# Score matmuls issued in front of the maxima matmuls within each attention step

## The chip, the cores and the metric

The kernel runs on one core of one Trainium2 chip. The metric is the time of one execution on the device in microseconds (us); the number given for a kernel is the median of several runs. TensorE is written PE below (its weight loads PEld), VectorE DVE, ScalarE ACT, GpSimd POOL, SyncE SP.

## What is computed

The reference is one layer of 16 sequences of 256 tokens, width 128, in float32: half a feed-forward block, attention, half a feed-forward block, each behind a layer norm and added to its input.

```python
x = x + 0.5 * ffn(layernorm(x))
x = x + attention(layernorm(x))        # 16 heads of 8 channels
x = x + 0.5 * ffn(layernorm(x))

# attention, for a batch of 256 tokens
scores = einsum('bhqd,bhkd->bhqk', q, k) * 8 ** -0.5
attn = softmax(scores, axis=-1)
o = einsum('bhqk,bhkd->bhqd', attn, v)
return einsum('bse,fe->bsf', o, Wo) + bo

# ffn, weights ternary with a scale per output
h = silu(lin(x, w1)) * lin(x, w2)
h = gelu(lin(h, h1)); h = gelu(lin(h, h2))
return lin(h, w3)
```

## The kernel before

All tokens stay in the tile `X`. The program has three stages: feed-forward over four blocks of 1024 tokens, attention over 16 batches of 256 tokens (one sequence each), feed-forward again. Each engine has its own instruction list, written out by hand, and they meet at semaphores only. Engines take their instructions in the order in which they are written.

**The softmax in two passes.** To subtract a row's maximum, the kernel computes the scores twice. The maxima matmuls (`max_scores`, line 1098) give scores with queries on the partitions; DVE reduces them to maxima (`max_unit`, line 828, the reduction at line 832). The negated maxima of a batch are turned by two PE transposes (`max_rows`, line 1136), and split into a high and a low part by ACT (line 657) and DVE (`split_max`, line 836, semaphore `m_lo`). The score matmuls (`scores`, line 1109) compute the scores a second time with keys on the partitions, and add the maxima through a selector matmul into the same bank; ACT takes the exponential (line 647). `weigh` (line 1121) multiplies the probabilities with the values.

**Units and steps.** A batch has 16 maxima units and 16 score units, each one PSUM bank of 128 x 512: two heads. A maxima unit is 2 matmuls (line 1104), a score unit 4 (lines 1116, 1118, twice). They contract over 32 rows only, one of four row groups ("lanes") of the array. `attend` for batch b has 16 steps u. Step u holds maxima unit u of the next batch, b + 1, and score unit u - 4 of batch b, or for u below 4 unit u + 12 of batch b - 1 (`in_step`, line 278). The lane of both is worked out from the unit's number, so that an even step and the odd step behind it use four different lanes: two for maxima, two for scores.

**Other work of a step.** At u = 3, 7, 11 and 15 stand two `weigh`s, 16 matmul records over all 128 rows. At u = 1 stands `max_rows`, at 3 `transpose_o`, at 5 `project_out`, at 13 `tokens_of_o`. An even batch up to 12 also has `project_v` at u = 9; an odd batch up to 11 has `transpose_att` at 7, `project_q` at 9 and `project_k` at 11, for the batches to come. All of this stands behind the matmuls of the step. All other steps, the even ones, hold nothing else.

**Banks and waits.** The maxima share three banks (`A_BANKS`), the scores three others (`B_BANKS`), so a maxima unit waits for DVE's reduction three units before (`max_done`, line 1102), a score unit for ACT's exponential three units before (`exp_done`, line 1113). At u = 4 score unit 0 also waits for `m_lo`. `transpose_att` waits for `att_added` (line 1330), which DVE's `add_att` (line 865) gives at its step 6. `max_rows` waits for `o_norm` of DVE's `scale_o` and for `max_twice` of POOL's `max_again` (line 444), which follows the last maxima of the batch.

DVE's order in a step is maxima unit, then the rest (`attend`, line 957): `split_max` at 2, layer norm's `normalise` at 3 in odd batches (line 770), `add_att` at 6, the norm statistics at 7 to 11 in even batches, `norm_o` at 14, `scale_o` at 15. ACT's order is in `attend`, line 663.

Of the kernel before, what the change touches and what calls it, by code (L numbers as in the profile page):

```python
# [53 lines left out]
A_BANKS = ((0, 1, 5) * 5 + (0,), (5, 1, 0) * 5 + (5,))  # L54
B_BANKS = ((2, 3, 7) * 5 + (2,), (7, 3, 2) * 5 + (7,))
ENTRY_BANKS = (0, 3, 1, 2) * 4
# [9 lines left out]
def macaron_kernel(nc, x, w_ffn, w_att, s12, sg, s3, bqk, bv, bo, eye, sel, low_rows, out):  # L66
# [11 lines left out]
    with ctx:  # L78
# [176 lines left out]
        def wait(eng, s, v):  # L255

            if not isinstance(v, int) or v > 0:
                eng.wait_ge(s, v)
# [10 lines left out]
        def a_unit(u):  # L269

            jj, lane = u // 2 % 2, 2 * (u // 4 % 2) + u % 2
            return u // 8, jj, lane

        def b_unit(v):

            return v // 8, v // 2 % 2, 2 * (v // 4 % 2) + v % 2

        def in_step(u, prev, own=True):


            at = [(0, u - SKEW)] if own else []
            if prev:
                at.append((1, u - SKEW + UNITS))
            return [(d, v) for d, v in at if 0 <= v < UNITS + 4]

        def used_last(banks, prev, u):


            before = prev + banks[:u]
            return next((d for d in range(1, len(before) + 1) if before[-d] == banks[u]), u + 1)  # L290

        def q_of(ring):

            return QK[:, RING - 1 - ring, 0, :, :]

        def k_of(ring):

            return QK[:, RING - 1 - ring, 1, :, :]
# [710 lines left out]
        def _(pe):  # L1009
# [88 lines left out]
            def max_scores(b, par, bb, u, banks, prev):  # L1098

                qt, jj, lane = a_unit(u)  # L1100
                rows = slice(32 * lane, 32 * lane + 32)
                wait(pe, max_done, UNITS * b + u - used_last(banks, prev, u) + 1)
                for i in range(2):
                    ins = MM(bank[banks[u]][:, SEQ * i:SEQ * i + SEQ],  # L1104
                             q_of(2 * par + bb)[rows, 2 * jj + i, P * qt:P * qt + P],
                             k_of(2 * par + bb)[rows, 2 * jj + i, :], start=True, stop=True)
                ins.then_inc(a_mm, 1)

            def scores(b, par, bb, v):

                jj, kt, lane = b_unit(v)
                rows = slice(32 * lane, 32 * lane + 32)
                wait(pe, exp_done, UNITS * b + v - used_last(B_BANKS[bb], B_BANKS[1 - bb], v) + 1 + CREDIT)
                for i in range(2):
                    dst = bank[B_BANKS[bb][v]][:, SEQ * i:SEQ * i + SEQ]
                    MM(dst, k_of(2 * par + bb)[rows, 2 * jj + i, P * kt:P * kt + P],  # L1116
                       q_of(2 * par + bb)[rows, 2 * jj + i, :], start=True, stop=False)
                    ins = MM(dst, SEL[rows, 2 * jj + i, :], m_parts[rows, bb, :], start=False, stop=True)  # L1118
                ins.then_inc(b_mm, 1)

            def weigh(b, par, bb, g, kt):


                pe.wait_ge(exp_done, UNITS * b + 4 * g + 2 * kt + 2 + CREDIT)
                if kt == 0 and g == 0:
                    wait(pe, o_out, b)
                for h in range(4):
                    col = BLOCK * (4 * g + h) + V_AT - VW * (g % 3)
                    ins = MM(bank[4][32 * h:32 * h + 32, SEQ * (g // 3):SEQ * (g // 3) + SEQ],  # L1129
                             V[par][:, VROW * (2 * bb + kt) + col:VROW * (2 * bb + kt) + col + BLOCK],  # L1130
                             probs[:, (4 * g + 2 * kt + h % 2) % 8, SEQ * (h // 2):SEQ * (h // 2) + SEQ],
                             start=kt == 0 and g in (0, 3), stop=kt == 1 and g >= 2, tile_position=(0, 32 * h))
                if kt == 1:
                    ins.then_inc(pv_mm, 1)

            def max_rows(b, bb):
                pe.wait_ge(max_twice, 2 * b + 2)
                for qt in range(2):
                    ins = T.transpose(bank[6][:, P * qt:P * qt + P],  # L1139
                                      neg_max[:, bb, qt, :], EYE[:, :])  # L1140
                ins.then_inc(m_T, 1)
# [9 lines left out]
            def transpose_o(b):  # L1151
                pe.wait_ge(o_norm, b + 1)
                for qt in range(2):
                    ins = T.transpose(bank[6][:, P * qt:P * qt + P], o_nat[:, qt, :], EYE[:, :])
                ins.then_inc(on_T, 1)
# [116 lines left out]
            def attend(b, pair, par, bb, prev=True, prev2=True, own=True, more=True, steps=UNITS,  # L1272
                       ahead=None, v_pair=None):

                npar, nbb = (par, 1) if bb == 0 else (1 - par, 0)
                ppar, pbb = (par, 0) if bb == 1 else (1 - par, 1)
                if more:  # L1280

                    of = pair + 1 - nbb
                    pe.wait_ge(qk_loaded[2 * npar + nbb], LOADS // 2 * (of - npar) + LOADS)
                def rows_of_max():
                    if prev2:
                        pe.wait_ge(o_norm, b - 1)
                    elif prev:
                        pe.wait_ge(v_set, pair + 2)
                    max_rows(b, bb)

                for u in range(steps):
                    if u == 0 and own and not prev:
                        pe.wait_ge(q_full, 1)
                        pe.wait_ge(k_full, 1)
                    if more:
                        max_scores(b + 1, npar, nbb, u, A_BANKS[nbb], A_BANKS[bb] if prev else ENTRY_BANKS)
                    for d, v in in_step(u, prev, own):
                        at = (b - d, par, bb) if d == 0 else (b - d, ppar, pbb)
                        if d == 0 and v == 0:
                            pe.wait_ge(m_lo, b + 1)  # L1300
                        if v < UNITS:
                            scores(*at, v)
                        if d == in_step(u, prev, own)[-1][0] and u == 1 and own:
                            rows_of_max()
                        if v >= 7 and v % 4 == 3:
                            weigh(*at, v // 4 - 1, 0)
                            weigh(*at, v // 4 - 1, 1)
                    if u == 1 and own and not prev:
                        pe.wait_ge(x_added, NB + CREDIT)
                        rows_of_max()  # L1310
                    if u == 3 and prev2:
                        if own:
                            pe.wait_ge(m_lo, b + 1)
                        else:
                            pe.wait_ge(o_norm, b - 1)
                        transpose_o(b - 2)
                    if u == 5 and prev2:
                        project_out(b - 2)
                    if u == UNITS - 1 and not more and own:
                        transpose_x(XN1, 0, 1)  # L1320
                        transpose_x(XN1 + 1, 1, 5)
                    if u == 9 and v_pair is not None:

                        if prev2:
                            pe.wait_ge(att_added, b - 1)
                        pe.wait_ge(m_lo, b + 1)
                        project_v(v_pair, 6)
                    if u == 7 and ahead is not None:
                        if prev2:
                            pe.wait_ge(att_added, b - 1)  # L1330
                        pe.wait_ge(m_lo, b + 1)
                        pe.wait_ge(v_set, pair + 2)
                        transpose_att(ahead, 0, 6)
                    if u == 9 and ahead is not None:
                        project_q(ahead, 6)
                    if u == 11 and ahead is not None:
                        pe.wait_ge(q_full, ahead)
                        project_k(ahead, 6)
                    if u == TOKENS and own and prev:

                        if ahead is not None:
                            pe.wait_ge(k_full, ahead)
                        elif v_pair is not None:
                            pe.wait_ge(v_set, v_pair + 1)
                        elif prev2:
                            pe.wait_ge(att_added, b - 1)
                        tokens_of_o(b - 1)
# [68 lines left out]
```

## Time and profile before

| | |
|---|---|
| median of 3 runs | 638.17 us (636.6 to 639.28) |
| the profiled execution's own time | 636.52 us |
| its span, first to last instruction | 634.7 us |
| granted TensorE clock, mean over the span | 0.986 |
| PE busy, of the span | 94% |
| ACT busy | 74% |
| DVE busy | 69% |
| POOL busy | 15% |

The profile is of one execution. The span is 1.8 us shorter than that execution's time, and that execution is 1.65 us below the median. Attention lies between about 219 and 445 us of the span. A timeline row gives a group of instructions: start in us from the span's start, length in us, engine, source line, operation, what it writes and reads, partitions x elements, the count, and in brackets the idle time of the engine before it with what ended it. Rows of PE overlap, as matmuls of different lanes run at the same time.

### The profile page before, as it was taken

The numbers are of one execution on the slowest core, as the hardware profiler recorded it, in microseconds if no ns is written. First come the engines' busy times: TensorE is split into PE (matmuls) and PEld (weight loads), VectorE is DVE, ScalarE is ACT, GpSimd is POOL, SyncE is SP. The second block draws the span as 40 slices with busy tenths as digits, with TensorE's granted clock in tenths as the row PEclk, the third lists the DMA queues.
The fourth block names the chain that finished last, engine by engine and source line by source line (L and its number), as shares of the span: only waits on it lengthen the run. The fifth ranks groups of instructions, "written<-read, shape, count | busy, mean of one in ns | idle before, by whom it ended". The sixth has DMA issues, their size and how long they took to land.

```text
span 634.7 us, 12980 instructions
## 1 busy us (share of the span) xinstructions
PE 597.0 (94%) x4452; PEld 437.7 (69%) x4452; DVE 436.8 (69%) x1034; ACT 466.7 (74%) x793; POOL 94.7 (15%) x258
## 2 busy tenths in 40 slices
PE   1959999999999999999999999999899999999996
PEld 0738878878776675656656565666578878788785
DVE  4845485667835687979889898896385666855742
ACT  2746796787875568787878878787587877977964
POOL 2702001021010311222222222012001020020000
PEclk9979999999999979999999999999899999999999
DMA  8200000000034073434437062400000001000011
GB/s 287 69 2 2 0 1 1 2 0 0 1 133 133 24 242 124 144 136 133 165 104 263 36 229 106 162 2 2 3 2 0 1 1 35 0 6 27 1 33 35
DMA packets 36674, 41.97 MB, mean 66 GB/s; under 512 B 2448, under 2 KB 27280, under 8 KB 36624
## 3 DMA queue, kind: packets, MB, share of 16 engines
q1 hardware_dynamic: 36624, 41.31, 19.3%
q8 instruction: 31, 0.51, 0.3%
q14 instruction: 19, 0.16, 0.1%
HBM read 22.42 MB, written 18.87 MB: 65 GB/s over the span
## 4 chain that ended last, share of the span: by engine, by line
PE 76%; DVE 8%; issue 7%; POOL 3%; ACT 3%; DMA 2%; POOLq 0%; SPq 0%; DVEq 0%; ACTq 0%
PE bank L1021 48%; PE bank L1129 7%; PE bank L1104 6%; PE bank L1116 3%; PE bank L1118 2%; DVE neg_max L832 2%; PE bank L1161 2%; PE bank L1086 1%; PE bank L1090 1%; DVE act_lo L782 1%; PE bank L1068 1%; PE bank L1147 1%; PE bank L1139 1%; DMA QK<-qk_scratch 1%; DVE silu L791 1%
## 5 line engine op out<-in xcount | busy, mean ns | idle before, releaser
L1021 PE MATMUL bank<-act_hi,WH 128*128 128x512 f32 x576 | 233.1, 405 | 6.6 <-issue 5.3
L1021 PE MATMUL bank<-act_lo,WH 128*128 128x512 f32 x576 | 228.3, 396 | 0.0
L832 DVE TENSOR_REDUCE neg_max<-bank 128x2 f32<-128x512 f32 x256 | 166.2, 680 | 31.8 <-PE bank L1104 30.2
L802 DVE TENSOR_TENSOR act_lo<-full,act_hi 128x512 fp32r<-128x512 f32 x128 | 87.8, 688 | 123.2 <-ACT act_hi L536 123.0
L647 ACT ACTIVATE probs<-bank 128x512 f32<-128x512 f32 x256 | 139.3, 597 | 34.1 <-PE bank L1118 32.3
L534 ACT ACTIVATE full<-bank,SG 128x512 f32<-128x512 f32 x128 | 88.1, 688 | 70.0 <-PE bank L1021 69.6
L1021 PEld LDWEIGHTS bank<-act_hi,WH 128*128 128x128 f32 x576 | 108.7, 189 | 36.8 <-issue 5.9
L1021 PEld LDWEIGHTS bank<-act_lo,WH 128*128 128x128 f32 x576 | 108.8, 189 | 25.1 <-issue 0.5
L1116 PE MATMUL bank<-QK 32*128 32x256 f32 x512 | 93.1, 331 | 0.9 <-DVE m_parts L838 0.5
L536 ACT ACTIVATE act_hi<-bank,SG 128x512 fp32r<-128x512 f32 x128 | 87.4, 683 | 0.0
L1118 PE MATMUL bank<-m_parts,SEL 32*128 32x256 f32 x512 | 79.3, 277 | 0.0
L1104 PE MATMUL bank<-QK 32*128 32x256 f32 x512 | 74.3, 331 | 1.8 <-DVE neg_max L832 1.2
L1104 PEld LDWEIGHTS bank<-QK 32*128 32x128 f32 x512 | 46.1, 185 | 40.4 <-issue 21.1
L1129 PE MATMUL bank<-probs,V 128*32 128x256 f32 x1024 | 69.9, 391 | 0.0
L1116 PEld LDWEIGHTS bank<-QK 32*128 32x128 f32 x512 | 61.4, 185 | 3.6 <-ACT probs L647 2.1
L1118 PEld LDWEIGHTS bank<-m_parts,SEL 32*128 32x128 f32 x512 | 61.9, 187 | 0.0
L791 DVE SCALAR_TENSOR_TENSOR silu<-bank,S,silu 128x512 f32<-128x512 f32 x64 | 47.1, 743 | 16.4 <-ACT silu L521 15.9
L1021 PE MATMUL bank<-x_hi,WH 128*128 128x512 f32 x128 | 51.7, 404 | 2.1 <-issue 1.6
L1021 PE MATMUL bank<-x_lo,WH 128*128 128x512 f32 x128 | 51.1, 399 | 0.0
L521 ACT ACTIVATE silu<-bank,S 128x512 f32<-128x512 f32 x64 | 43.1, 683 | 9.5 <-PE bank L1021 9.5
L399 POOL TENSOR_TENSOR newton<-rstd 128x8 f32<-128x8 f32 (+1 forms) x45 | 11.9, 265 | 241.0 <-DVE rstd L762 238.7
L782 DVE TENSOR_TENSOR act_lo<-silu,act_hi 128x512 fp32r<-128x512 f32 x64 | 45.5, 710 | 0.2
(91 smaller groups left out, 593.2 us busy)
## 6 DMA issues: line engine op xcount, KB each, us to landing
qk_scratch<-qk SPq DMA_DIRECT2D x64, 256.0 KB, 2.6
QK<-qk_scratch SPq DMA_DIRECT2D x16, 1024.0 KB, 7.1
X<-x SPq DMA_DIRECT2D x4, 512.0 KB, 7.2
raw_rest<-w_ffn SPq DMA_DIRECT2D x4, 512.0 KB, 6.0
out<-X SPq DMA_DIRECT2D x4, 512.0 KB, 3.2
raw<-w_ffn SPq DMA_DIRECT2D x3, 256.0 KB, 4.5
WA<-w_att SPq DMA_DIRECT2D x1, 256.0 KB, 5.4
xT<-sel SPq DMA_DIRECT2D x1, 256.0 KB, 5.4
```

The costliest lines, as they stand in the source:

```text
L534: A.activation(full[:, t, :], bank[4 + t % 2][:, :], ACT.Gelu, scale=SG[:, layer, t:t + 1])
L536: A.activation(act_hi[1 + layer][:, j, t, :], bank[4 + t % 2][:, :], ACT.Gelu, scale=SG[:, layer, t:t + 1]).then_inc(g_hi, 1)
L647: A.activation(probs[:, v % 8, :], bank[B_BANKS[bb][v]][:, :], ACT.Exp, scale=SCALE)\
L782: D.tensor_tensor(act_lo[0][:, t // HT, t % HT, :], silu[:, t % SLOTS, :], act_hi[0][:, t // HT, t % HT, :].bitcast(F32), op=ALU.subtract)\
L791: D.scalar_tensor_tensor(out=silu[:, t % SLOTS, :], in0=bank[UP_BANKS[t]][:, :], scalar=S12[:, 1, t % HT:t % HT + 1], in1=silu[:, t % SLOT ...
L802: D.tensor_tensor(act_lo[1 + layer][:, j, t, :], full[:, t, :], act_hi[1 + layer][:, j, t, :].bitcast(F32), op=ALU.subtract)\
L832: D.tensor_reduce(neg_max[:, bb, qt, n0:n0 + 2], bank[(banks or A_BANKS[bb])[u]][:, :].rearrange("p (h k) -> p h k", h=2), axis=AX.X, op=A ...
L1021: ins = MM(dst, a, b, start=k == 0, stop=k == len(todo) - 1)
L1104: ins = MM(bank[banks[u]][:, SEQ * i:SEQ * i + SEQ], q_of(2 * par + bb)[rows, 2 * jj + i, P * qt:P * qt + P], k_of(2 * par + bb)[rows, 2 * ...
L1116: MM(dst, k_of(2 * par + bb)[rows, 2 * jj + i, P * kt:P * kt + P], q_of(2 * par + bb)[rows, 2 * jj + i, :], start=True, stop=False)
L1118: ins = MM(dst, SEL[rows, 2 * jj + i, :], m_parts[rows, bb, :], start=False, stop=True)
L1129: ins = MM(bank[4][32 * h:32 * h + 32, SEQ * (g // 3):SEQ * (g // 3) + SEQ], V[par][:, VROW * (2 * bb + kt) + col:VROW * (2 * bb + kt) + c ...
```

## The change

In `attend` of PE's list the loop over `in_step` is split in two. The first part, with the wait for `m_lo` and the score matmuls, now stands ahead of `max_scores`; the second part, with `rows_of_max` and the `weigh`s, stays behind it. No instruction is added or taken away, and no other engine's list changes.

```diff
                     if u == 0 and own and not prev:
                         pe.wait_ge(q_full, 1)
                         pe.wait_ge(k_full, 1)
-                    if more:
-                        max_scores(b + 1, npar, nbb, u, A_BANKS[nbb], A_BANKS[bb] if prev else ENTRY_BANKS)
                     for d, v in in_step(u, prev, own):
                         at = (b - d, par, bb) if d == 0 else (b - d, ppar, pbb)
                         if d == 0 and v == 0:
                             pe.wait_ge(m_lo, b + 1)
                         if v < UNITS:
                             scores(*at, v)
+                    if more:
+                        max_scores(b + 1, npar, nbb, u, A_BANKS[nbb], A_BANKS[bb] if prev else ENTRY_BANKS)
+                    for d, v in in_step(u, prev, own):
+                        at = (b - d, par, bb) if d == 0 else (b - d, ppar, pbb)
                         if d == in_step(u, prev, own)[-1][0] and u == 1 and own:
                             rows_of_max()
                         if v >= 7 and v % 4 == 3:
```

## Rows read from the trace of the kernel before

**Rows 1.** The page's first line: the span.

```profile
span 634.7 us, 12980 instructions
```

**Rows 2.** Waits in the attention stretch: total us, times, longest.

```profile
ACT probs L647 <- PE bank L1118: 30.5, 67, 1.2
DVE neg_max L832 <- PE bank L1104: 27.4, 40, 1.5
...
PEld bank L1139 <- POOL neg_max L450: 3.7, 8, 0.6
...
PEld bank L1139 <- DVE o_nat L861: 2.0, 6, 0.8
```

**Rows 3.** Busy time in two batches: PE, PEld, DVE, ACT, POOL, clock, DMA.

```profile
302.40:331.10 28.70, 28.11 (x365) 17.96 (x368) 24.99 (x64) 23.27 (x45) 7.15 (x20) 1.00 0.43 149
```

**Rows 4.** Timeline of PE: steps 0 and 1 of an even batch.

```profile
307.57 0.38 PE L1104 MATMUL bank<-QK 32*128 32x256 f32 x1
307.57 0.38 PE L1116 MATMUL bank<-QK 32*128 32x256 f32 x1
307.59 0.38 PE L1104 MATMUL bank<-QK 32*128 32x256 f32 x1
...
308.03 0.29 PE L1118 MATMUL bank<-m_parts,SEL 32*128 32x256 f32 x2
```

**Rows 5.** Timeline of PE: steps 6 and 7 of an odd batch.

```profile
325.82 0.38 PE L1104 MATMUL bank<-QK 32*128 32x256 f32 x1
...
326.26 0.38 PE L1104 MATMUL bank<-QK 32*128 32x256 f32 x1
326.26 0.38 PE L1116 MATMUL bank<-QK 32*128 32x256 f32 x1
...
326.48 0.27 PE L1104 MATMUL bank<-QK 32*128 32x256 f32 x1
...
326.93 0.42 PE L1129 MATMUL bank<-probs,V 128*32 128x256 f32 x4
```

**Rows 6.** Timeline of DVE: steps 2 to 6 of the same batch.

```profile
323.57 0.41 DVE L838 TENSOR_TENSOR m_parts<-bank,m_top 128x256 fp32r<-128x256 f32 x1
...
324.50 1.11 DVE L770 TENSOR_SCALAR xn<-X,moments,rstd 128x128 f32 x4
325.52 1.88 DVE L832 TENSOR_REDUCE neg_max<-bank 128x2 f32<-128x512 f32 x3
327.32 0.41 DVE L868 TENSOR_TENSOR X<-bank,X 128x256 f32 x1
```

**Rows 7.** Timeline of ACT: exponentials of steps 4 and 5 there.

```profile
325.35 1.09 ACT L647 ACTIVATE probs<-bank 128x512 f32<-128x512 f32 x2 [0.37 <-PE bank L1118]
```

**Rows 8.** Timeline of PE: the transposes behind step 7 there.

```profile
327.94 0.66 PE L1081 MATMUL bank<-EYE,xn 128*128 128x128 f32 x4
```

**Rows 9.** Timeline of PE, ACT, DVE: steps 2 and 3 of an even batch.

```profile
308.84 0.38 PE L1104 MATMUL bank<-QK 32*128 32x256 f32 x1
...
308.99 0.38 PE L1104 MATMUL bank<-QK 32*128 32x256 f32 x2
...
309.08 0.39 PE L1116 MATMUL bank<-QK 32*128 32x256 f32 x2
...
308.42 1.09 ACT L647 ACTIVATE probs<-bank 128x512 f32<-128x512 f32 x2 [0.60 <-PE bank L1118]
...
310.38 0.68 DVE L832 TENSOR_REDUCE neg_max<-bank 128x2 f32<-128x512 f32 x1
```

**Rows 10.** Timeline of the first batch: DVE from step 3, PE at step 4.

```profile
223.66 3.07 DVE L832 TENSOR_REDUCE neg_max<-bank 128x2 f32<-128x512 f32 x5
223.80 0.38 PE L1116 MATMUL bank<-QK 32*128 32x256 f32 x1 [0.49 <-DVE m_parts L838]
...
230.19 0.69 DVE L832 TENSOR_REDUCE neg_max<-bank 128x2 f32<-128x512 f32 x1 [1.07 <-PE bank L1104]
```

**Rows 11.** Timeline of PE: step 7 of the second batch.

```profile
240.21 0.38 PE L1104 MATMUL bank<-QK 32*128 32x256 f32 x1 [0.72 <-DVE neg_max L832]
```

## The prediction

> **What bounds the kernel now.** The page comes first, for the span [rows 1]; only attention is touched. I then read the waits of the attention stretch [rows 2]: ACT idles 30.5 us for score matmuls, DVE 27.4 us for maxima matmuls. So neither consumer is the bound alone. In two batches, 28.70 us, DVE is busy 24.99, ACT 23.27 and PE 28.11 [rows 3]: PE's list is nearly the whole path, with some holds in it. To see which holds the swap can touch, one has to look at single matmuls.
>
> A pair of steps (even, then odd) without a hold looks like this [rows 4]: the even step's maxima matmul starts at 307.57, its score matmul at 307.57, the odd step's maxima matmul at 307.59, and the last selector matmuls of both at 308.03. The reader is to see two things. All four lanes run side by side, so the pair's length is that of the longer lane, a score lane with four matmuls, the last of which starts 308.03 - 307.57 = 0.46 us behind the first. And the odd step's maxima matmul starts at 307.59 although the even step's last score matmuls, written ahead of it, start at 308.03: a lane's matmul doesn't wait for the matmuls of another lane. A wait on a semaphore does hold back everything that is written behind it.
>
> So the swap matters in two ways: the order of issue within a step, which is worth about 0.01 us (307.57 against 307.59 is all that the whole even step takes to issue), and who is held behind whose wait.
>
> **Holds that the change removes.** In the kernel before, a maxima unit that waits for DVE holds back a score unit that is ready. In odd batches this happens at step 7. Step 6 starts at 325.82, step 7 only at 326.26, maxima and scores together [rows 5], 0.44 later where 0.02 is regular. DVE is late because of the layer norm: `normalise` takes 324.50 to 325.52, and the three reductions behind it go in one stretch of 1.88 us [rows 6]; the first of them, unit 4, is the one that frees the bank, at about 325.52 + 0.68 = 326.20. The score unit needs the exponential of step 4, the first of two that begin at 325.35 and take 1.09 [rows 7], so it is free at about 325.95. With scores in front they start at 325.95 to 326.00, about 0.27 earlier.
>
> What is the pair's end worth then? Behind it `weigh` starts at 326.93, 0.67 after the score unit and 0.45 after the second maxima matmul of 326.48 [rows 5]. In a regular pair a 128-row operation follows the last matmul's start of a lane by about 0.2 (326.93 against a last selector matmul at 326.26 + 0.46 = 326.72). Scores: 326.00 + 0.67 = 326.67. Maxima, unmoved: 326.48 + 0.20 = 326.68. So `weigh` starts near 326.68, a gain of 0.25 us.
>
> **What is late next.** Behind `weigh` stand the transposes, at 327.94 [rows 8], and they wait for `add_att`, which ends at 327.32 + 0.41 = 327.73 [rows 6]. DVE is in one stretch from `split_max` to there, so this doesn't move. With about 0.05 to 0.1 to take the semaphore they can start at 327.80 to 327.85. Of the 0.25 us, about 0.10 is left. That holds for batches 3, 5, 7, 9 and 11: 5 x 0.10 = 0.50 us. Bounds for each: 0 (if taking the semaphore and the waits behind it costs 0.2) and 0.25 (if it were no wait).
>
> Batch 1 has the same hold at step 7, 240.21 with an idle PE of 0.72 before it [rows 11], and there `transpose_att` doesn't wait for `add_att` (there is no batch two before it): the full 0.25 us.
>
> **Holds that stay.** In even batches step 3 is held twice: its maxima unit starts at 308.99 instead of 308.86, then its score unit at 309.08 [rows 9]. The score unit waits for the exponential of step 0, which begins at 308.42 and ends near 309.02. With scores in front they still start at 309.08, and the pair ends where it did: 0. Steps 7 and 15 of even batches repeat this with the score unit as the late one, as do steps 3 of the odd batches. Nothing is won in any of them.
>
> **What it adds.** Where the score unit is the late one, the maxima unit is now held behind it, here from 308.99 to about 309.09, 0.10. Its second matmul is 0.22 behind the first and takes 0.28, so DVE could read near 309.6; DVE takes this unit at 310.38 [rows 9], as it has `split_max` and a unit before it. The cover is 0.8 us, and at steps 7 and 15 the order of DVE's list (`add_att`, `norm_o`) gives a like one. I cost this at 0. If the cover went, the price would be the held time, 0.1 to 0.2 each, three times a batch in eight batches: 2.4 to 4.8 us.
>
> The wait for `m_lo` at step 4 now stands ahead of a maxima unit too, 16 times. `split_max` is done at 323.57 + 0.41 = 323.98 [rows 6], and step 4 comes behind `weigh` and `transpose_o`, at about the time `normalise` starts, 324.50: free by 0.5. Only in the first batch does it bind. There step 4's scores wait until 223.80, and the maxima unit, issued ahead of them now, would wait too. DVE runs units 3 to 7 in a stretch from 223.66 [rows 10], so wants unit 4 at 223.66 + 0.6 = 224.26 and would have it at 223.81 + 0.22 + 0.28 = 224.31 or a little more: a loss of up to 0.1 on DVE. It idles 1.07 before 230.19 [rows 10], so the loss ends there: 0, at most 0.1.
>
> **Order of issue.** Each pair's scores start about 0.01 earlier, its maxima about 0.01 later. The chain between batches runs over both: maxima to DVE to `max_rows` about three times in two batches, scores to the end of a pair about four times. They cancel: 0, within 0.3 us either way. SP, POOL and the DMAs keep their lists, and nothing is moved past a queue of theirs.
>
> **The sum** is 0.50 + 0.25 = 0.75 us off. Against the profiled execution, 636.52, that is 635.8; its time is 1.65 below the median of 638.17, so as a median it is 637.4 us, 0.1% faster. A measurement of this kernel can tell about 0.5%, 3.2 us, from no change.
>
> **Rival A: the maxima fall behind the scores, slower.** If a maxima matmul issued behind four score matmuls starts only when the last of those has, it comes 0.46 us later [rows 4]. DVE waits for maxima 40 times [rows 2], and a delay of DVE reaches PE again at `max_rows`, which waits for POOL's doubled maxima 8 times and for DVE's `o_nat` 6 times [rows 2], and at `add_att`: three links in two batches, seven times. 3 x 7 x 0.46 = 9.7 us: 647.8 us. It decides from a lag of 0.15 us of maxima behind scores (3.2 us / 21). Against it: in [rows 4] the odd step's maxima matmul overtakes two matmuls of the even step's scores that have not started.
>
> The Trainium skill (page "TensorE: Matmul & The Clock Gate", part 3, "The mechanism") says that packed matmuls start and end in program order, with no reordering. By that rule rival A would hold and the sum would be 647.8 instead of 637.4. The trace disagrees with it, by those 0.44 us between 307.59 and 308.03.
>
> **Rival B: the holds count in full, faster.** If the transposes aren't limited by `add_att` and the maxima lane doesn't end the pair, step 7 gives its whole 0.44 in six odd batches, 2.6 us, and if the 0.15 us of step 3 in seven even batches goes too, 1.1 more: 3.7 us off, 634.5 us. Against it: the maxima unit itself can't start before 326.26, and the score unit of step 3 not before 309.08.
>
> **Rival C: nothing moves.** The semaphore's taking eats the 0.10, and batch 1's gain is lost in a later wait for DVE: 638.2 us.
>
> **How the numbers follow.** My forecast of a small gain gets 0.70 and rival C 0.15; both are within 0.5%. Rival B gets 0.08, rival A 0.07. The range goes from 635.2, the two bounds of the forecast in its favour (1.5 us) and some of B with the spread of medians, to 639.8, which takes in rival C, 0.4 us of added waits and a median as far from the next as the runs of before are (1.1 us above). Chances: faster 0.08, same 0.85, slower 0.07.
>
> **What would show it.** In the changed profile: step 7 of odd batches has its score matmul 0.25 us ahead of its maxima matmul; `weigh` follows the maxima by 0.67 - 0.22 = 0.45 or less; the transposes follow `add_att`'s end by about 0.1; two batches take 28.6 instead of 28.70 us. In even batches steps 3, 7 and 15 have maxima just behind late scores, and DVE's stretches don't change. The idle times of DVE and ACT for PE stay within 1 us. It is wrong if maxima matmuls lag scores by over 0.1 us in pairs without a hold, if DVE idles more at steps 3, 7 or 15, or if the time between batches changes by more than 0.3 us.

## The result, and the profile after

The changed kernel takes 640.88 us (median of 9 runs, 640.2 to 642.91), the kernel before in the same comparison 638.69 (9 runs, 636.6 to 639.28). The ratio on record is 1.0055, with a 95% interval of 1.0036 to 1.0075: slower, by about 3.5 us; the two medians as they stand are 2.2 us apart. 637.4 was predicted, with a range from 635.2 to 639.8.

The page of the changed kernel, its span and the row of the granted clock in 40 slices:

```profile
span 638.9 us, 12980 instructions
...
PEclk9979999999999979999999999999999999999999
```

The span grew by 4.2 us [rows 1]. Waits between 219 and 445 us, as in [rows 2] (who waited for whom: us in total, times, longest):

```profile
DVE neg_max L832 <- PE bank L1104: 31.2, 45, 1.5
...
ACT probs L647 <- PE bank L1118: 29.2, 65, 1.2
...
PEld bank L1154 <- DVE m_parts L838: 8.4, 14, 0.6
...
PEld bank L1139 <- POOL neg_max L450: 6.2, 8, 0.9
...
PEld bank L1139 <- DVE o_nat L861: 3.6, 6, 1.0
```

ACT waits no longer than before: 29.2 here and 30.5 up to 449 us, where this kernel's attention ends, against 30.5. DVE waits 3.8 us more (27.4) [rows 2], and PE waits more behind DVE and POOL: 6.2 for 3.7, and 3.6 for 2.0 [rows 2]. In the kernel before, the row of `transpose_o` waiting for `m_parts` was this:

```profile
PEld bank L1154 <- DVE m_parts L838: 5.8, 14, 0.4
```

So the time went where a delay of DVE reaches PE. Busy time hardly moves: in two batches, now 29.4 us long, DVE is busy 25.06 and PE 27.79, where it was 24.99 and 28.11 in 28.70 us [rows 3].

```profile
302.40:331.80 29.40, 27.79 (x360) 17.46 (x360) 25.06 (x63) 23.52 (x44) 7.15 (x20) 1.00 0.42 145
```

**A measure for what follows.** Attention repeats itself every two batches: in the trace of the kernel before to within 0.03 us from batch 1 to batch 12, while whole runs of one kernel differ by several us. In other kernels the early batches differ by more, in the odd-step kernel below from 28.37 to 28.60 us. So I compare the kernels by the time between the same instruction in batches 6 and 8: DVE's `split_max`. First the kernel before (the timeline of DVE), then the changed one:

```profile
310.05 0.41 DVE L838 TENSOR_TENSOR m_parts<-bank,m_top 128x256 fp32r<-128x256 f32 x1
...
338.75 0.41 DVE L838 TENSOR_TENSOR m_parts<-bank,m_top 128x256 fp32r<-128x256 f32 x1
```

```profile
312.35 0.41 DVE L838 TENSOR_TENSOR m_parts<-bank,m_top 128x256 fp32r<-128x256 f32 x1
...
341.77 0.41 DVE L838 TENSOR_TENSOR m_parts<-bank,m_top 128x256 fp32r<-128x256 f32 x1
```

That is 28.70 against 29.42 us, 0.72 more. Over the seven pairs of batches from 1 to 14 it makes 5.0 us at most, as the last batches have less to do. From the first `split_max` to the last, the trace has 211.16 us before (223.33 to 434.49) and 215.53 with the change (223.60 to 439.13): 4.4 us, so all that the span grew by lies in attention.

**Where the 0.72 comes from.** Steps 4 and 5 of batch 6, PE's timeline of the changed kernel, then DVE's first reduction of these maxima:

```profile
313.18 0.38 PE L1116 MATMUL bank<-QK 32*128 32x256 f32 x1
313.20 0.38 PE L1104 MATMUL bank<-QK 32*128 32x256 f32 x1
...
313.22 0.38 PE L1104 MATMUL bank<-QK 32*128 32x256 f32 x1
...
313.42 0.28 PE L1104 MATMUL bank<-QK 32*128 32x256 f32 x1
...
313.64 0.29 PE L1118 MATMUL bank<-m_parts,SEL 32*128 32x256 f32 x2
```

```profile
314.00 0.69 DVE L832 TENSOR_REDUCE neg_max<-bank 128x2 f32<-128x512 f32 x1 [0.64 <-PE bank L1104]
```

The maxima matmuls of step 4 aren't held: the first starts at 313.20, the second at 313.42, and by their rows they end at 313.70. But DVE, idle for 0.64 us, starts only at 314.00, 0.80 after the first maxima matmul. In the kernel before it was 0.54, for the same step:

```profile
311.11 0.38 PE L1104 MATMUL bank<-QK 32*128 32x256 f32 x1
```

```profile
311.64 0.69 DVE L832 TENSOR_REDUCE neg_max<-bank 128x2 f32<-128x512 f32 x1 [0.58 <-PE bank L1104]
```

What now stands in front of the maxima in the list is the score unit, whose last matmul is the first of the two that start from 313.64 on; with the usual 0.27 it ends at about 313.91. DVE starts 0.09 behind that end, as it started 0.04 behind the end of the maxima before.

**When the semaphore is updated.** In these traces the end of a matmul's row is modelled. But they also record the time of every semaphore update, from which the views infer who ended a wait, and there the 0.26 us can be read without any model. In the kernel before, the maxima of this step update `a_mm`, for which DVE waits, at 311.619, 0.014 behind the end of their row. In the changed kernel they update it at 313.972, 0.274 behind it; the score unit in front of them has updated its own semaphore, `b_mm`, at 313.929. Over all even steps of batches 2 to 14 the median distance from the row's end to the update is 0.014 us before and 0.281 with the change, and wherever DVE has idled for these maxima it starts 0.02 behind the update. In both kernels all 416 updates of the two semaphores from steps of this stretch come in the order of the program, the closest 0.042 apart. The maxima of odd steps, which stand behind the even step's score unit in both kernels, are 0.279 late in the kernel before already.

### The profile page after: what moved, and what is told of

It is laid out like the page before. It is cut to its first block, busy times and chain, and to the rows that moved or that the text cites. A ratio compares the mean times of both kernels' runs of the same rounds, so it can differ in the third digit from the quotient of the medians.

```text
span 638.9 us, 12980 instructions
## 1 busy us (share of the span) xinstructions
PE 593.2 (93%) x4452; PEld 433.4 (68%) x4452; DVE 437.6 (68%) x1034; ACT 467.8 (73%) x793; POOL 94.9 (15%) x258
## 4 chain that ended last, share of the span: by engine, by line
PE 73%; issue 8%; DVE 8%; ACT 4%; POOL 3%; DMA 2%; POOLq 0%; SPq 0%; DVEq 0%; ACTq 0%
PE bank L1021 48%; PE bank L1116 6%; PE bank L1129 4%; PE bank L1104 2%; PE bank L1118 2%; DVE neg_max L832 2%; ACT probs L647 2%; PE bank L1161 2%; PE bank L1086 1%; PE bank L1090 1%; DVE act_lo L782 1%; PE bank L1068 1%; PE bank L1147 1%; PE bank L1154 1%; DVE silu L791 1%
## 5 line engine op out<-in xcount | busy, mean ns | idle before, releaser
L1116 PE MATMUL bank<-QK 32*128 32x256 f32 x512 | 89.6, 331 | 2.6 <-ACT probs L647 1.5
L1116 PEld LDWEIGHTS bank<-QK 32*128 32x128 f32 x512 | 59.0, 185 | 39.1 <-ACT probs L647 25.7
L1104 PE MATMUL bank<-QK 32*128 32x256 f32 x512 | 81.5, 331 | 0.8 <-DVE neg_max L832 0.4
L1118 PE MATMUL bank<-m_parts,SEL 32*128 32x256 f32 x512 | 75.7, 277 | 0.0
L1118 PEld LDWEIGHTS bank<-m_parts,SEL 32*128 32x128 f32 x512 | 59.7, 187 | 0.0
L1104 PEld LDWEIGHTS bank<-QK 32*128 32x128 f32 x512 | 52.3, 185 | 5.7 <-issue 3.6
```

Source lines behind the costliest of these rows:

```text
L1104: ins = MM(bank[banks[u]][:, SEQ * i:SEQ * i + SEQ], q_of(2 * par + bb)[rows, 2 * jj + i, P * qt:P * qt + P], k_of(2 * par + bb)[rows, 2 * ...
```

## The experiments

The experiments were set up on two theories, ahead of the reading of the semaphore updates. Theory 1: lanes run side by side, but other engines are told of the end of a matmul in the order of the program. A maxima unit written behind a score unit reaches DVE with the end of the score unit, 0.26 us late. Theory 2: the waits that now stand in front of the maxima hold them back. All kernels below compute the whole of the reference's output. "Two batches" is the measure above.

| kernel | two batches, us | against before |
|---|---|---|
| before | 28.70 | |
| the change | 29.42 | +0.72 |
| scores in front in odd steps | 28.60 | -0.10 |
| in even steps | 29.52 | +0.82 |
| maxima behind two of four score matmuls | 28.62 | -0.08 |
| behind three | 28.87 | +0.17 |
| waits alone in front | 28.88 | +0.18 |
| scores in front at steps 2, 6, 12, 14 | 29.52 | +0.82 |
| at steps 0, 4, 8, 10 | 28.96 | +0.26 |
| at step 2 | 29.01 | +0.31 |
| at step 6 | 28.97 | +0.27 |
| at steps 12, 14 | 29.01 | +0.31 |
| odd steps, `add_att` earlier | 28.37 | -0.33 |
| `add_att` earlier alone | 28.58 | -0.12 |

### Odd steps, even steps

```diff
+                    first = u % 2 == 1
-                    if more:
+                    if more and not first:
                         max_scores(b + 1, npar, nbb, u, A_BANKS[nbb], A_BANKS[bb] if prev else ENTRY_BANKS)
...
+                    if more and first:
+                        max_scores(b + 1, npar, nbb, u, A_BANKS[nbb], A_BANKS[bb] if prev else ENTRY_BANKS)
```

For the even steps `first` is `u % 2 == 0`.

> Scores in front of the maxima in odd steps only. Theory 1 (the end of a matmul is told to other engines in program order, so a maxima unit written behind a score unit reaches DVE only with the end of that score unit, about 0.26 us late, and this counts only where DVE waits for PE, which is in even steps): the loss is gone, two batches take 28.6 to 28.7 us as before, the time is within 0.3% of the kernel before. Theory 2 (the waits for the exponentials, now in front of the maxima in steps 3, 7 and 15, hold the maxima back and cost the time): those are odd steps, so the whole loss stays, two batches take 29.4 us and the time is 0.5 to 0.7% above before.

> Scores in front of the maxima in even steps only, the mirror of the run with odd steps. Theory 1 (ends told in program order): the whole loss stays, 29.4 us for two batches, 0.5 to 0.7% above before, and DVE takes the maxima of an even step at least 0.80 us after their first matmul starts where it waits for them, instead of 0.54. Theory 2 (waits in front of the maxima): exponentials are never late in even steps, so nothing is lost: 28.7 us for two batches.

Odd steps: 637.62 us (10 runs) against 637.05 for the kernel before (23 runs), ratio 1.001 (0.9981 to 1.0038), and 28.60 us for two batches. Even steps: 644.88 us (4 runs), ratio 1.0138 (1.0102 to 1.0174), and 29.52 us. The late exponentials are all in odd steps, the loss is all in even ones: for them theory 2 has fallen. Its other wait, for `m_lo` at step 4, is in an even step; the next experiment settles that one. The two parts add up: -0.10 and +0.82 make the 0.72 of the change. In the kernel with even steps, PE and DVE at step 4 of batch 6:

```profile
314.70 0.39 PE L1104 MATMUL bank<-QK 32*128 32x256 f32 x2
```

```profile
315.51 0.69 DVE L832 TENSOR_REDUCE neg_max<-bank 128x2 f32<-128x512 f32 x1 [0.65 <-PE bank L1104]
```

That is 0.81, as expected, and the updates of `a_mm` for even steps come 0.281 behind the row's end, as in the changed kernel (0.014 in the odd-step kernel). The 1.4% of the whole run is above the 0.5 to 0.7% expected, and more than 7 x 0.82 us, which is 0.9%. A part of the rest is the granted clock, told further down.

### How far behind: after two or three of the four score matmuls

```diff
     for i in range(2):
         dst = bank[B_BANKS[bb][v]][:, SEQ * i:SEQ * i + SEQ]
         MM(dst, k_of(2 * par + bb)[rows, 2 * jj + i, P * kt:P * kt + P],
            q_of(2 * par + bb)[rows, 2 * jj + i, :], start=True, stop=False)
+        if between is not None and 2 * i + 1 == behind:
+            between()
         ins = MM(dst, SEL[rows, 2 * jj + i, :], m_parts[rows, bb, :], start=False, stop=True)
...
+        if between is not None and 2 * i + 2 == behind:
+            between()
```

`between` issues the step's maxima. The score unit's waits, that for `m_lo` at step 4 too, stay in front of them. The cut line of the diff is the update of `b_mm`, which stays with the last score matmul.

> The score unit's wait and its first two matmuls stand in front of the maxima, its last two behind them. Theory 1 (ends told in program order): the maxima's end is told right behind that of the second score matmul, which ends about 0.50 us after the start, as the maxima do; DVE starts at 0.55 to 0.60 instead of 0.80, and two batches take 28.7 to 28.9 us, the time within 0.3% of before. Theory 2 (waits in front of the maxima): all waits stand where the change has them, so the whole loss stays, 29.4 us for two batches, 0.5 to 0.7% above before.

> As the run with the maxima behind two of the four score matmuls, but behind three. Theory 1 (ends told in program order): the third score matmul ends about 0.61 us after the start, so DVE takes the maxima at 0.68 to 0.72 where it waits for them (0.54 before, 0.80 with the change), and two batches take 29.0 to 29.15 us. Theory 3 (only the last score matmul, which gives the semaphore, delays what is behind it): 28.6 to 28.7 us.

Behind two: 637.53 us (10 runs), ratio 1.0011 (0.9987 to 1.0035), and 28.62 us for two batches. PE and DVE at step 4 of batch 6:

```profile
309.96 0.38 PE L1104 MATMUL bank<-QK 32*128 32x256 f32 x1
```

```profile
310.51 0.69 DVE L832 TENSOR_REDUCE neg_max<-bank 128x2 f32<-128x512 f32 x1 [0.57 <-PE bank L1104]
```

Behind three (one run, 637.16 us), the same step:

```profile
311.77 0.38 PE L1104 MATMUL bank<-QK 32*128 32x256 f32 x1
```

```profile
312.43 0.69 DVE L832 TENSOR_REDUCE neg_max<-bank 128x2 f32<-128x512 f32 x1 [0.49 <-PE bank L1104]
```

DVE starts 0.54, 0.55, 0.66 and 0.80 us behind the first maxima matmul with 0, 2, 3 and 4 score matmuls in front of it. Score matmuls of a lane start about 0.11 apart, and the delay grows with each one by that, from the third on; the first two end no later than the maxima do. The third one updates no semaphore, and it delays DVE all the same: so it is the order of ends, not the semaphore of the unit in front. The updates of `a_mm` say the same: 0.014, 0.025, 0.144 and 0.281 behind the row's end (medians of the even steps). I had expected 0.68 to 0.72, and 29.0 to 29.15 for two batches; 0.66 and 28.87 are short of it. A delay of 0.12 costs 0.27 against the odd-step kernel, which has the gain of step 7 too, where one of 0.26 costs 0.82. Such a small delay may be partly covered; that wasn't followed.

### The waits alone

```diff
+                    for d, v in in_step(u, prev, own):
+                        at = (b - d, par, bb) if d == 0 else (b - d, ppar, pbb)
+                        if d == 0 and v == 0:
+                            pe.wait_ge(m_lo, b + 1)
+                        if v < UNITS:
+                            scores_wait(*at, v)
                     if more:
                         max_scores(b + 1, npar, nbb, u, A_BANKS[nbb], A_BANKS[bb] if prev else ENTRY_BANKS)
```

`scores` no longer waits itself.

> Only the waits move: the waits for m_lo and for the exponentials stand in front of the maxima matmuls, the score matmuls behind them as before. Theory 1 (ends told in program order): DVE gets the maxima as before, two batches take 28.7 us, the time within 0.3% of before. Theory 2 (waits in front of the maxima): the whole loss, 29.4 us for two batches, 0.5 to 0.7% above before. Here the gain of scores that overtake late maxima at step 7 of odd batches is absent too.

639.6 us (8 runs), ratio 1.0039 (1.0017 to 1.0061), and 28.88 us for two batches: a miss for both theories, 0.18 above before, a quarter of the change's loss. Step 3 of batch 6, PE's timeline and then ACT's with the exponential that frees the bank, the first of two:

```profile
313.00 0.37 PE L1104 MATMUL bank<-QK 32*128 32x256 f32 x1
313.00 0.38 PE L1115 MATMUL bank<-QK 32*128 32x256 f32 x1
```

```profile
312.27 1.09 ACT L647 ACTIVATE probs<-bank 128x512 f32<-128x512 f32 x2 [0.69 <-PE bank L1117]
```

The exponential ends near 312.87, 0.6 behind its start, and the scores start 0.13 later; in the kernel before, 308.42 + 0.60 = 309.02 and 309.08, 0.06 later [rows 9]. Here two waits stand in front of one matmul, and the trace's instruction list has 116 of the waits for `max_done` as instructions of their own, where the kernel before has 7; the other 245 there are carried by the weight load of a maxima matmul. That such a wait takes longer to pass, I take for the 0.18; it is argued from these two places and wasn't tried by itself. The announcements aren't it: the updates of `a_mm` in even steps come 0.014 behind the row's end, as before. The run with the maxima behind two score matmuls has the scores' waits in the places where the change has them, 251 of its 252 waits for `max_done` are carried, and it loses nothing. So the waits' place costs nothing.

### Which steps count

`first` from above is `u in (2, 6, 12, 14)`, `u in (0, 4, 8, 10)`, `u == 2`, `u == 6` and `u in (12, 14)`, one run each.

> Scores in front at steps 2, 6, 12 and 14 only. Theory 1 with the chain read from the trace (DVE's lateness reaches PE through m_lo and max_rows only, and so from the maxima of these steps): two batches take 29.45 to 29.55 us, all that the run with all even steps lost. If every even step counts alike: about 29.1.

> Scores in front at steps 0, 4, 8 and 10 only, the other half of the even steps. Theory 1 with the chain read from the trace: 28.65 to 28.8 us for two batches, as before, though DVE starts 0.26 us later where it waits at these steps. If every even step counts alike: about 29.1.

> Scores in front at step 2 only. Theory 1 with the chain read from the trace: DVE is 0.26 late with the maxima of step 2, so with split_max, and PE's transpose_o behind step 3 waits for m_lo: about 0.26 in odd batches, where DVE waits for this unit, and 0.1 to 0.2 in even ones; two batches take 29.0 to 29.15 us.

> Scores in front at step 6 only. Theory 1 with the chain read from the trace: DVE waits for this unit in even batches, and the norm's steps, POOL's Newton steps and max_again follow it up to PE's max_rows in the odd batch: 0.2 to 0.26, two batches take 28.9 to 28.95 us.

> Scores in front at steps 12 and 14 only. Theory 1 with the chain read from the trace: DVE is 0.26 late with the unit of step 14 in odd batches, so with norm_o and scale_o, for which max_rows of the even batch waits: 0.2 to 0.26; in even batches POOL's Newton steps, not DVE, hold max_rows, so nothing there. Two batches take 28.9 to 28.95 us.

The four steps of the chain lose all that the even steps lose, 29.52. Alone, step 2 costs 0.31, step 6 0.27 and steps 12 and 14 together 0.31, 0.89 in sum, a little more than together; the last two lie 0.02 and 0.06 above what was expected. The other four steps missed their expectation: 28.96 instead of at most 28.8. Their 0.26 arises in even batches. DVE's timeline from step 4 of batch 6, and PE's first maxima matmul of step 7:

```profile
316.27 1.89 DVE L832 TENSOR_REDUCE neg_max<-bank 128x2 f32<-128x512 f32 x3 [0.86 <-PE bank L1104]
```

```profile
317.02 0.38 PE L1104 MATMUL bank<-QK 32*128 32x256 f32 x1
```

The maxima of step 4 come 0.26 late, DVE has reduced them at about 316.27 + 0.68 = 316.95, and step 7, whose bank they free, starts at 317.02 instead of with step 6. Step 6 had started at 316.78, and an odd step starts 0.02 behind it when nothing holds it. A late start of DVE needn't pass `max_rows` to be felt: the ring of three banks hands it to PE three steps on.

That bears on step 6 too, for which I had expected the way over POOL and `max_rows`. With step 6 alone in front, the loss is on PE already at step 11 of batch 6, whose bank comes free with DVE's reduction of unit 8:

```profile
317.61 0.67 DVE L832 TENSOR_REDUCE neg_max<-bank 128x2 f32<-128x512 f32 x1
```

```profile
318.34 0.38 PE L1104 MATMUL bank<-QK 32*128 32x256 f32 x1
```

The reduction ends at 318.28, step 10 had started at 318.11 and step 11 starts at 318.34; in the kernel before they started at 316.06 and 316.08. So these runs show which steps count, not by which wait each of them reaches PE.

The times of the whole runs don't follow the measure here: 643.83, 643.90, 641.21, 639.19 and 639.95 us, in the order of the table, beside 637.08 (17 runs) for the kernel before with the first two and 635.96 (one run) with the others. The second takes as long as the first with 0.56 us less in two batches. A part of that is the granted clock: between 236 and 250 us its trace has 0.76 and that of the first 1.00, between 219 and 236 us 0.80 and 0.70.

### A faster version

The change's own gain, scores that pass late maxima at step 7 of odd batches, is in the odd-step kernel: 0.10 in two batches. `weigh` and the transposes behind step 7 there, and DVE's `add_att`:

```profile
326.46 1.07 PE L1129 MATMUL bank<-probs,V 128*32 128x256 f32 x16
327.64 0.54 PE L1081 MATMUL bank<-EYE,xn 128*128 128x128 f32 x3
```

```profile
327.10 0.41 DVE L868 TENSOR_TENSOR X<-bank,X 128x256 f32 x1
```

`weigh` is done with its issue about 1.0 later, at 327.46; the transposes wait until 327.64, for the end of `add_att` at 327.51. So it was taken forward on DVE.

```diff
+                    if u == 6 and prev2:
+                        add_att(b - 2, 2 * b - 4)
                     if more:
                         max_unit(b + 1, 1 - bb, u)
                     if u == 2:
                         split_max(b, bb)
-                    if u == 6 and prev2:
-                        add_att(b - 2, 2 * b - 4)
```

> Scores in front in odd steps, and DVE adds the attention's output to X ahead of the maxima of step 6 instead of behind them. Theory 1 and the prediction's own step (of the 0.25 us won at step 7 of odd batches, 0.15 is lost to the wait for add_att): the transposes behind step 7 follow weigh without a wait, two batches take 28.35 to 28.5 us, against 28.6 with odd steps alone and 28.7 before; the time is 0.2 to 0.4% below before, 1.3 to 2.5 us. If another wait takes its place: 28.6 and no difference to the run with odd steps.

> Only DVE's part: add_att ahead of the maxima of step 6, PE's list as in the kernel before. If what the combination won (28.37 us for two batches against 28.59 with odd steps alone) comes only from the transposes behind step 7 of odd batches, nothing is won here, since PE is held by late maxima until then: 28.65 to 28.7 us. If taking add_att forward wins by itself (its time before step 7, or m_lo and max_rows further on): 28.45 to 28.5 us.

With odd steps: 636.10 us (12 runs, 634.67 to 639.51) against 637.08 (17 runs), ratio 0.9979 (0.9953 to 1.0005), and 28.37 us for two batches, 0.33 less than before. Its rows:

```profile
325.24 1.07 PE L1129 MATMUL bank<-probs,V 128*32 128x256 f32 x16
326.25 0.55 PE L1081 MATMUL bank<-EYE,xn 128*128 128x128 f32 x3
```

```profile
325.19 0.41 DVE L868 TENSOR_TENSOR X<-bank,X 128x256 f32 x1
```

The transposes follow `weigh` by 1.01, without a wait. Over seven pairs 0.33 makes 2.3 us, and the measured difference of the medians is 1.0; the interval just holds no change, so as a time of the whole kernel this is likely, not shown. `add_att` alone wins 0.12 in two batches, more than the nothing and less than the 0.2 that I had as its two cases; that part wasn't followed further. Its one run took 637.29 us, beside one of 635.96 of the kernel before, so as a whole run it shows no gain.

### The granted clock

The kernels' times hold some us that the two-batch measure doesn't. In the kernel before, the stretch behind attention (windows: length, busy of PE, PEld, DVE, ACT, POOL, granted clock, DMA) is partly at the lower of the two levels, 1.2 instead of 2.4 GHz:

```profile
445.00:460.00 15.00, 12.33 (x89) 8.14 (x86) 5.07 (x12) 8.66 (x15) 0.73 (x1) 0.89 0.01 3
```

A share of 0.89 of 15 us is 3.3 us at half clock; in the changed kernel's profile this window has 1.00. It cost the kernel before little: from the last `split_max` to the first matmul of the third stage it took 20.27 us (434.49 to 454.76), the changed kernel 19.79 (439.13 to 458.92). The kernel with the waits alone has a fall in its second batch, where the kernel before has 1.00:

```profile
236.00:250.00 14.00, 13.20 (x129) 7.67 (x122) 8.81 (x17) 9.16 (x17) 0.66 (x2) 0.76 0.01 3
```

The kernel with even steps shows 0.88 there. These falls are one reason why a ratio can stand above or below what the two-batch measure gives. Whether the order of the matmuls brings them about is open; it wasn't tried.

## Why the prediction was wrong

**The step that failed** is "Order of issue": "They cancel: 0, within 0.3 us either way." It rested on the sentence that a lane's matmul doesn't wait for the matmuls of another lane. That is true of its start, and I read it as true of what DVE is told. Measured, the maxima reach DVE 0.26 us later than in the kernel before, not 0.01, and it costs 0.82 us in two batches, 0.72 together with the gain of step 7. The kernel before doesn't show this in a wait for the maxima: its maxima stood first in the pair, and the odd step's maxima, which do stand behind a score unit, are taken by a DVE that is still busy with the even step's. It does show it in its semaphore updates, which I hadn't read: 0.279 behind the row's end in odd steps, 0.014 in even ones. Of the prediction's signs of being wrong, the time between batches (0.72, the limit was 0.3) and the idle time of DVE (3.8 more, the limit was 1) told; the lag of the maxima behind the scores, 0.02 in a pair without a hold, didn't, as it is one of starts.

**Rival A** had 0.07 and was the nearest: maxima held behind the scores. Its mechanism was wrong in the start (they start on time) and right in the end; its lag was 0.46 where 0.26 was measured, so its 9.7 us were too many. The changed kernel's waits bear out its links: `max_rows` behind POOL (6.2 us for 3.7) and behind `o_nat` (3.6 for 2.0), and a third one. That I had put at `add_att`; it is `m_lo`, for which `transpose_o` waits, after step 2 (8.4 for 5.8). Its threshold of 0.15 was passed. The rule of the Trainium skill (page "TensorE: Matmul & The Clock Gate", part 3, "The mechanism"), that packed matmuls start and end in program order, was set aside because the starts disagree with it. They do, here too. For the ends, as other engines see them, the DVE starts, 0.54 to 0.80, and the order of the semaphore updates agree with it. A rule with two halves has to be tested on both.

**Step 7 of odd batches** went as predicted. PE's timeline of the changed kernel, batch 7, and DVE's:

```profile
328.53 0.38 PE L1116 MATMUL bank<-QK 32*128 32x256 f32 x1
...
328.88 0.38 PE L1104 MATMUL bank<-QK 32*128 32x256 f32 x1
...
329.31 0.64 PE L1129 MATMUL bank<-probs,V 128*32 128x256 f32 x8
```

```profile
329.94 0.41 DVE L868 TENSOR_TENSOR X<-bank,X 128x256 f32 x1
```

```profile
330.48 0.65 PE L1081 MATMUL bank<-EYE,xn 128*128 128x128 f32 x4
```

The scores lead the maxima by 0.35, `weigh` follows the maxima by 0.43 (0.45 or less was predicted), and the transposes follow the end of `add_att`, 330.35, by 0.13 (about 0.1). The 0.10 us that I left of 0.25 is what the odd-step kernel gains from batch 5 on; before that it gains more, 0.31 from batch 1 to 3 (28.37 for 28.68 us), with the step 7 for which 0.25 was predicted, and 0.21 from batch 3 to 5. In the change it is lost under the 0.82.

**Holds that stay, and the cover of 0.8 us** at steps 3, 7 and 15: right, as far as the time tells. The odd-step kernel holds the maxima back at all three and loses nothing. **The wait for `m_lo`** in front of maxima: the kernel with the maxima behind two score matmuls has it in that place and takes no longer than before. Rivals B and C didn't come about.

## What to carry to other kernels

Small matmuls in separate row groups overlap, but in these traces their results are announced in the order of the program: write the short unit that an idle engine waits for in front, even when both start in the same 0.02 us. Where the engine is still busy, as with the odd steps' maxima here, the order costs nothing. Before moving an instruction that starts early anyway, ask who is told of its end, and read that from the consumer's start, in a place where the consumer is idle, or from the semaphore's update. A gain that one wait leaves over (0.25 us here) is capped by the next one: taking `add_att` forward as well brought the odd-step kernel from 28.60 to 28.37.

## What the hardware showed that was not expected

- A matmul whose row ends at 313.70 lets DVE start at 314.00 when a matmul of another lane, written in front of it, ends at 313.91. With 0, 2, 3 and 4 such matmuls in front, DVE starts 0.54, 0.55, 0.66 and 0.80 us behind the first maxima matmul, and its semaphore is updated 0.014, 0.025, 0.144 and 0.281 us behind the row's end.
- All 416 updates of `a_mm` and `b_mm` that were compared, in the kernel before and in the changed one, come in the order of the program, though the matmuls start out of it.
- Starts don't follow the program's order across lanes: the odd step's first maxima matmul starts 0.02 us behind the even step's (313.20 and 313.22 in the changed kernel's timeline), while the even step's last selector matmul, written ahead of both, starts at 313.64.
- With the waits written as instructions of their own in front of other matmuls, the score unit of one step started 0.13 us behind the end of the exponential, against 0.06 in the kernel before, where the weight load of its first matmul carried the wait.
